# Rotary attention: scores computed a second time with keys on partitions, and four heads summed in one bank

## The chip, the cores and the metric

The kernel runs on one core of a Trainium2 chip. The metric is the device time of one execution in microseconds (us). The core has TensorE (PE; its weight loads are listed as PEld), VectorE (DVE), ScalarE (ACT), GpSimd (POOL) and SyncE (SP), which run side by side and wait for each other through semaphores. TensorE writes only to PSUM, eight banks of 512 f32 columns on 128 partitions.

## The reference

Four token sequences of 576 tokens (64 image patches and 512 text tokens) with 64 features go through four layers, each of an attention and a feed-forward part. The change lies in the attention of the second layer's feed-forward block, a causal softmax attention with rotary positions, 4 heads of 16 features (k and v are shared by two heads each):

```python
q = q * cos + _rotate_half(q) * sin
k = k * cos + _rotate_half(k) * sin
scores = jnp.einsum('bhtd,bhsd->bhts', q, k) / jnp.sqrt(jnp.float32(HD))
scores = jnp.where(causal[None, None], scores, jnp.float32(-1e+30))
att = jax.nn.softmax(scores, axis=-1)
y = jnp.einsum('bhts,bhsd->bhtd', att, v).transpose(0, 2, 1, 3).reshape(Bx, Tx, Cx)
x = x + y @ wo.T
```

The other parts (a linear attention, a retrieval attention over a table of keys, a Toeplitz layer by transforms, the experts after this attention, a sparse attention, a tree of small layers, a sigmoid attention, experts) are not touched.

## The kernel before

The kernel is a row of stages. A stage opens one or more blocks; in a block every engine runs its own list of instructions in the order in which it is written, and a barrier of all engines ends the block. There is no planner: the order within each list and the semaphores between lists are written out by hand. Tokens lie on partitions: a sequence is 5 tiles (CH) of 128 tokens, the last of 64 (TAIL), and there are 20 tiles (T) in all. SEQ is 576, P 128, D 64, BANK 512, HD 16.

`rotary_experts_stage` (line 2058) norms the input, makes qkv by one product, turns q and k by the rotary tables on DVE, and then runs these stages in turn:

- `stack_parts_stage` (line 2010): every q and k value is cut into bf16 parts, and six of them are laid side by side, so that a bf16 product over 6 x 16 = 96 (PARTS) features gives nearly f32 scores. ACT, POOL and DVE share the copies; POOL waits for the first cast before its own four.
- `causal_attention_stage` (line 926), called "rot_soft", with `CausalAttention` (from line 691). For each of 16 heads (4 sequences of 4) POOL copies q, k and v of the head into small tiles. TensorE turns q and k (line 785) so that features lie on partitions, and DVE copies them out of PSUM (line 801). For each tile c of 128 queries TensorE makes the scores against the (c+1) x 128 keys up to them (lines 811 and 813), DVE adds the mask and takes the row's maximum in one instruction (line 913) and scales it (line 916), ACT takes the exponential with the row's sum (line 881), TensorE turns the exponentials block by block (line 823, f32), ACT copies them to SBUF (line 871), and TensorE weighs v: the turned exponentials are the stationary operand and 16 columns of v the moving one (line 836). DVE divides by the sum (lines 893, 896). TensorE's list interleaves the next head's turn and first scores with this head's. DVE, ACT and TensorE run these lists as hardware loops over pairs of heads.
- a fill of the lower half of yT (line 688), and `turn_stage` (line 301), which turns the attention's result, so that features lie on partitions (lines 315, 324, 332).
- `product_stage` (line 336) for the output projection, which adds to core.xn (lines 354, 2099).

Another attention, `RetrievedAttention` (line 1005), is a subclass of `CausalAttention` with f32 scores and 64 features; it stays as it is.

Of the kernel before, what the change touches and what calls it, by code (L numbers as in the profile page):

```python
# [21 lines left out]
BF16 = mybir.dt.bfloat16  # L22
ACT = mybir.ActivationFunctionType
AX = mybir.AxisListType

P = 128
B = 4
PATCHES = 64
TEXT = 512
SEQ = PATCHES + TEXT  # L30
D = 64
CH = 5
PAD = CH * P
TAIL = SEQ - 4 * P
T = B * CH
COLS = T * P
BANK = 512
GROUPS = COLS // BANK
LN_EPS = 1e-5
NEG = -1e30  # L40
# [641 lines left out]
def set_stage(nc, name, fills):  # L682

    with nc.Block() as block:
        @block.gpsimd
        def _(pool):
            for ap, value in fills:
                nc.gpsimd.memset(ap, value)


class CausalAttention:
# [213 lines left out]
    def dve_head(self, dve, steps, n, u, more, carry, out_of, out_before=None):  # L905
# [15 lines left out]
                self.dve_turn(dve, n + 1, 1 - u, c == 2)  # L921
        if not more:
            self.dve_norm(dve, steps, n, u, out_of)


def causal_attention_stage(nc, core, name, sources, out, heads, d, scale, parts=None):

    with Stage(nc, name) as st:  # L930
        A = CausalAttention(nc, core, st, d, scale, parts=parts)
        widths = (A.dq, A.dq, d)
        vec = st.sem("vector_steps")
        A.begin()
        pairs = heads // 2
        views = lambda b, h: [of[:, bass.ds(b * CH, CH), bass.ds(h * stride + start, w)]
                              for (of, stride, start), w in zip(sources, widths)]
        out_of = lambda b, h: (lambda lo, hi, r: out[0:r, bass.ds(b * CH + lo, hi - lo), bass.ds(h * d, d)])

        def walk(engine, pair):  # L940

            def sequence(b, first=False, last=False):
                for j in range(pairs):
                    pair(b, j, first and j == 0, last and j == pairs - 1)

            sequence(0, first=True)
            with engine.Fori(1, B - 1) as b:
                sequence(b)
            sequence(B - 1, last=True)

        with nc.Block() as block:
            @block.gpsimd
            def _(pool):
                with pool.Fori(0, B) as b:
                    with pool.Fori(0, pairs) as j:
                        for u in range(2):
                            A.pool_fetch(pool, b * heads + j * 2 + u, u, *views(b, j * 2 + u))

            @block.tensor
            def _(pe):  # L960
                A.pe_start(pe, 0, 0)
                with pe.Fori(0, B * pairs - 1) as m:
                    for u in range(2):
                        A.pe_head(pe, m, u, True)
                for u in range(2):
                    A.pe_head(pe, B * pairs - 1, u, u == 0)

            @block.scalar
            def _(act):
                with act.Fori(0, B * pairs) as m:  # L970
                    for u in range(2):
                        A.act_head(act, 2 * m + u, u)

            @block.vector
            def _(dve):
                steps = Steps(dve, vec)

                def pair(b, j, first, last):
                    n, h = b * heads + j * 2, j * 2

                    steps.before, steps.count = A.STEPS * n - (0 if first else 2), 0
                    if first:
                        A.dve_start(dve, n, 0)
                    before = None if first else out_of(b, h - 1) if h else out_of(b - 1, heads - 1)
                    A.dve_head(dve, steps, n, 0, True, not first, out_of(b, h), before)
                    A.dve_head(dve, steps, n + 1, 1, not last, True, out_of(b, h + 1), out_of(b, h))

                walk(dve, pair)


KEYS = 64
# [924 lines left out]
Q_HEADS = 4  # L1916
HD = D // Q_HEADS
# [87 lines left out]


PARTS = 6 * HD


def stack_parts_stage(nc, qkv, q_parts, k_parts):  # L2010


    with Stage(nc, "parts") as st:
# [9 lines left out]
        with nc.Block() as block:  # L2023
# [13 lines left out]

            @block.gpsimd
            def _(pool):
                pool.wait_ge(cast, 1)  # L2040
                place(nc.gpsimd.tensor_copy, q_parts, 4, 0, 0)
                for column in (0, 2, 5):
                    place(nc.gpsimd.tensor_copy, k_parts, column, 0, 1)
# [14 lines left out]
def rotary_experts_stage(nc, core, I, norm):  # L2058


    with Stage(nc, "rot") as st:
        spare = st.sb("spare", [P, T, D])
        with Stage(nc, "rot_attn") as at:
# [13 lines left out]
            with Stage(nc, "rope") as rt:  # L2077
                vec = rt.sem("vector_steps")
                with nc.Block() as block:
                    @block.vector  # L2080
                    def _(dve):
# [3 lines left out]
                        for b in range(B):  # L2085
                            for lo, table in parts:
# [2 lines left out]
                                    table[:, :, :].unsqueeze(2).to_broadcast([P, CH, 2 * Q_HEADS, HD]), ALU.mult))  # L2089
                        steps.settle()  # L2090
                        steps.do(nc.vector.tensor_tensor(qkv[:, :, 0:2 * D], qkv[:, :, 0:2 * D], qkv[:, :, 2 * D:4 * D], ALU.add))
            q_parts, k_parts = (at.sb(n, [P, T, Q_HEADS * PARTS], BF16) for n in ("q_parts", "k_parts"))
            stack_parts_stage(nc, qkv, q_parts, k_parts)
            causal_attention_stage(nc, core, "rot_soft", [(q_parts, PARTS, 0), (k_parts, PARTS, 0), (qkv, HD, 4 * D)], qkv,
                                   Q_HEADS, HD, HD ** -0.5, parts=PARTS)
            set_stage(nc, "rot_padding", [(yT[D:P, :], 1.0)])
            turn_stage(nc, core, "rot_turn", [(yT, D, lambda t: qkv[:, t, 0:D])])
            product_stage(nc, core, "rot_proj", [(lambda t: yT[:, t * P:(t + 1) * P], w_out[:, :])], D,
                          lambda t0, t1, made: nc.vector.tensor_tensor(core.xn[:, t0:t1, :], core.xn[:, t0:t1, :], made, ALU.add))
        router, weight = st.sb("router", [P, T, EXPERTS]), st.sb("weight", [P, T, EXPERTS])  # L2100
# [849 lines left out]
```

## Time and profile before

| | us |
|---|---|
| median of three runs | 4470.99 (4460.36 to 4479.04) |
| the profiled execution | 4491.15 |
| its span | 4489.0 |
| TensorE busy | 3640.8 (81%) |
| DVE busy | 2651.9 (59%) |
| ACT busy | 1496.4 (33%) |
| POOL busy | 359.1 (8%) |

Shares of busy time are means over a row of very different stages. The rotary attention is about a twentieth of the span, so it is read from the stretch in which it runs. Busy time of TensorE counts products in flight, and products overlap: where the time that a product occupies TensorE matters, it is the distance from its start to the next one's. "PEclk" and the granted clock of a stretch are TensorE's clock as a share of full speed: 1.00 is 2.4 GHz, 0.50 is 1.2 GHz.

### The profile page before, as it was taken

The page shows a single profiled execution, that of the slowest core. Times are in us where ns is not written, and L with a number is a line of the kernel's source. Part 1 is how long each engine was busy: PE and PEld are TensorE (multiplying, and loading weights), DVE is VectorE, ACT ScalarE, POOL GpSimd, SP SyncE. Part 2 cuts the span into 40 slices and gives each one's busy share as a digit, 9 for nine tenths or more (in the row PEclk, how much of TensorE's full clock was granted, in tenths as well). Part 3 has the DMA queues.
Part 4 walks back from the last instruction along what each step waited for, and adds up shares of the span by engine and source line. Part 5 has one row for each costly group of instructions (what it writes and reads, how often), then busy time and mean ns, then how long its engine had stood idle before and what let it go on. Part 6 is the DMA issues. An engine that isn't in the chain of part 4 may idle for free. (4 is left out here: it accounts for less than half of the span.)

```text
span 4489.0 us, 57158 instructions
## 1 busy us (share of the span) xinstructions
PE 3640.8 (81%) x16965; PEld 2172.9 (48%) x17110; DVE 2651.9 (59%) x7758; ACT 1496.4 (33%) x2931; POOL 359.1 (8%) x351
## 2 busy tenths in 40 slices
PE   5528889999999999999799868848869372799867
PEld 4325545544454554444466645437747252344354
DVE  3369878777887877555333322144344555899812
ACT  2203444444444444444333330034432133100023
POOL 1000000000000000000000001111000000355500
PEclk8569999999999999999878877975579665899968
DMA  0102334443443444443000020000010002100000
GB/s 7 52 10 76 102 87 102 87 91 86 101 92 83 101 88 91 107 104 71 24 19 20 21 79 0 0 4 1 1 31 0 1 0 54 43 0 0 0 7 5
DMA packets 140950, 207.83 MB, mean 46 GB/s; under 512 B 35104, under 2 KB 119657, under 8 KB 135469
## 3 DMA queue, kind: packets, MB, share of 16 engines
q1 hardware_dynamic: 140717, 205.03, 19.1%
q8 instruction: 108, 1.77, 0.2%
q14 instruction: 125, 1.02, 0.1%
HBM read 115.66 MB, written 10.03 MB: 28 GB/s over the span
## 5 line engine op out<-in xcount | busy, mean ns | idle before, releaser
L1256 PE MATMUL psum<-pk_W,pk_kv 128*128 128x512 f32 (+1 forms) x2560 | 1203.8, 552 | 10.0 <-issue 9.8
L1487 DVE SCALAR_TENSOR_TENSOR pk_W<-psum,pk_E 128x512 f32<-128x512 f32 (+1 forms) x1280 | 810.5, 633 | 440.3 <-ACT pk_E L1354 407.2
L1354 ACT ACTIVATE pk_E<-psum 128x512 f32<-128x512 f32 (+1 forms) x1280 | 708.8, 554 | 1005.0 <-PE psum L1246 1003.1
L1256 PEld LDWEIGHTS psum<-pk_W,pk_kv 128*128 128x128 f32 x2560 | 465.4, 191 | 173.7 <-issue 27.0
L1245 PE MATMUL psum<-pk_stack,pk_spread 128*128 128x512 bf16 (+1 forms) x1171 | 420.4, 359 | 80.0 <-DVE pk_W L1487 53.6
L1246 PE MATMUL psum<-pk_stack,pk_spread 128*128 128x512 bf16 (+1 forms) x1280 | 459.4, 359 | 17.7 <-DMA pk_stack<-pk_marks 9.5
L2480 PE MATMUL psum<-tree_w,tree_x 128*128 128x512 bf16 x1692 | 381.0, 380 | 112.9 <-PEq L120 90.7
L1245 PEld LDWEIGHTS psum<-pk_stack,pk_spread 128*128 128x128 bf16 x1280 | 125.1, 98 | 444.8 <-DVE pk_W L1487 349.4
L2480 PEld LDWEIGHTS psum<-tree_w,tree_x 128*128 (+1 forms) x1728 | 168.2, 99 | 312.0 <-issue 121.3
L2551 DVE COPY_PREDICATED leaf_acc<-leaf_path,psum 128x512 f32<-128x512 uint32 x468 | 310.4, 729 | 5.1 <-PE psum L2480 2.8
L1246 PEld LDWEIGHTS psum<-pk_stack,pk_spread 128*128 128x128 bf16 x1280 | 125.7, 98 | 241.8 <-issue 232.0
L1220 PEld LDWEIGHTS psum<-pk_ranked,pk_onehot 128*128 128x128 bf16 x2304 | 168.3, 149 | 115.4 <-issue 102.8
L1220 PE MATMUL psum<-pk_ranked,pk_onehot 128*128 128x128 bf16 x2304 | 172.1, 230 | 56.9 <-DVE pk_onehot L1445 56.9
L1190 POOL TENSOR_TENSOR pk_parts<-pk_left,pk_parts 128x512 bf16<-128x512 f32 (+1 forms) x40 | 44.0, 1100 | 1814.9 <-ACT pk_parts L1325 1814.9
L1441 DVE TENSOR_TENSOR pk_onehot<-pk_idf,pk_count 128x2048 bf16<-128x2048 bf16 x144 | 175.4, 1218 | 1.2 <-PE psum L1220 0.6
L295 PE MATMUL psum<-ident,xn 128*64 128x128 f32 x160 | 34.2, 407 | 171.7 <-DVEq L269 157.6
L881 ACT ACTIVATE peer_probs<-peer_probs,peer_stat 128x128 f32<-128x128 f32 (+4 forms) x160 | 96.3, 602 | 222.9 <-DVE peer_stat L916 222.7
L811 PE MATMUL psum<-peer_kv,peer_qT_padded 128*128 128x128 f32 (+4 forms) x320 | 163.3, 603 | 5.9 <-DVE peer_v L1051 3.5
L913 DVE CUSTOM_DVE_ANT_0 peer_probs<-psum,peer_mask 128x128 f32<-128x128 f32 (+4 forms) x160 | 85.9, 537 | 116.2 <-PE psum L811 106.2
L1957 PE MATMUL psum<-moe_x,moe_w 128*85 x480 | 113.8, 388 | 43.6 <-PEq L120 42.3
L1061 PE MATMUL psum<-peer_v,peer_pT 128*128 128x64 f32 (+2 forms) x960 | 139.4, 289 | 0.0
L1061 PEld LDWEIGHTS psum<-peer_v,peer_pT 128*128 128x128 f32 (+2 forms) x960 | 123.7, 202 | 20.7 <-issue 15.3
(513 smaller groups left out, 4970.1 us busy)
## 6 DMA issues: line engine op xcount, KB each, us to landing
pk_kv<-in_kv SPq DMA_DIRECT2D x40, 2048.0 KB, 7.8
pk_stack<-pk_parts SPq DMA_DIRECT2D x768, 64.0 KB, 2.5
pk_stack<-pk_marks SPq DMA_DIRECT2D x256, 64.0 KB, 2.6
peer_kv<-peer_kept SPq DMA_DIRECT2D x32, 288.0 KB, 2.8
peer_kept<-pk_made SPq DMA_DIRECT2D x32, 256.0 KB, 2.1
tree_weights_x<-in_tree_w SPq DMA_DIRECT2D x32, 256.0 KB, 4.6
pk_stack<-pk_parts SPq DMA_DIRECT2D x192, 32.0 KB, 2.0
dft_cos<-in_cos SPq DMA_DIRECT2D x1, 2596.5 KB
```

The costliest lines, as they stand in the source:

```text
L811: last = nc.tensor.matmul(ps[0:r, bank, 0:min(w, BANK)], q, self.kT[:, u, 0:min(w, BANK)], start=True, stop=True)
L1061: last = nc.tensor.matmul(ps[0:r, 1, c * d:(c + 1) * d], self.pT[0:k, self.pT_at[c] + m * r:self.pT_at[c] + (m + 1) * r], self.v1[0:k, u, ...
L1220: last = nc.tensor.matmul(ps[:, 6 + h // 4, h % 4 * P:(h % 4 + 1) * P], onehot[:, h % 2, :, :, r], ranked[:, r, :], start=(r == 0), stop=( ...
L1245: nc.tensor.matmul(ps[:, n % 2, 0:N], spread[:, 1, c % 2, :], of, start=True, stop=True)
L1246: nc.tensor.matmul(ps[:, 2 + n % 2, 0:N], spread[:, 0, c % 2, :], of, start=True, stop=True).then_inc(x_made, 1)
L1256: nc.tensor.matmul(ps[:, 4, 0:N], kv[:, k % 2, c, :], W[:, n % 3, 0:N], start=(c == 0), stop=(c == CHUNKS - 1)).then_inc(acc_done, 1)
L1354: nc.scalar.activation(E[:, n % 2, 0:width(k)], ps[:, 2 + n % 2, 0:width(k)], ACT.Exp).then_inc(e_made, 1)
L1441: steps.do(nc.vector.tensor_tensor(onehot[:, h % 2, :, :, :], idf[:, :, h, :].unsqueeze(2).to_broadcast([P, 2, KEYS, TOP]), count64[:, :, ...
L1487: nc.vector.scalar_tensor_tensor(W[:, n % 3, 0:width(k)], ps[:, n % 2, 0:width(k)], TOP + 0.5, E[:, n % 2, 0:width(k)], ALU.is_gt, ALU.mul ...
L1957: last = nc.tensor.matmul(ps[0:HALF, 3 * which + u % 3, :], w[:, lo:lo + HALF], x[:, bass.ds(g * BANK, BANK)], start=(k == 0), stop=(k == 2))
L2480: last = nc.tensor.matmul(ps[:, n % BANKS, :], x[:, bass.ds(t * P, P)], w[:, c * BANK:(c + 1) * BANK], start=(k == 0), stop=(k == len(prod ...
L2551: ins = nc.vector.copy_predicated(acc[:, u, level + 1, :, :], over(mask.bitcast(U32), D), bank)
```

## The change

`causal_attention_stage` goes, and with it the fill and the turn stage behind it. `rotary_attention_stage` takes its place. For each head n:

- TensorE turns q and k as before, straight from the stacked parts, which now have a stride of 128 (Q_STRIDE) instead of 96; ACT copies them out of PSUM (two copies) instead of DVE.
- First scores, queries on partitions, and DVE's masked maximum as before, but with nothing after it: DVE's instruction writes its sums to a scratch tile and keeps the maximum.
- DVE writes the negative maximum as two bf16 pieces into two of the 32 spare columns of the stacked q parts (`piece`); the spare columns of k hold 1. TensorE turns these q tiles again (`turn_peaks`), and DVE copies the rows 96 to 127 into the turned q (`copy_peaks`). A contraction over all 128 rows then gives score minus maximum.
- Second scores with keys on partitions (`score_turned`): three banks per head hold all key blocks against the queries from them on; the causal mask is added by TensorE as a product of an identity with a bf16 mask. ACT takes three exponentials of 512 columns, PSUM to SBUF.
- Weighing (`weigh`): v is the stationary operand, 128 columns wide (its head's 16 columns at the head's place among 64, zeros beside them, and ones at 64 columns further), and the exponentials are the moving operand in f32. All four heads of a sequence accumulate in bank 1, with values in rows 0 to 63 and sums in rows 64 to 127, already turned. The first 64 queries go to a piece of bank 2.
- After each fourth head DVE takes the reciprocal of the sums and multiplies into yT (`norm`); the first weighing of the next sequence waits for it.

The lists are written out over all 16 heads in place of the hardware loops. POOL fills v for two sequences at a time and sets the spare columns and yT in `stack_parts_stage`, ahead of its wait for the cast.

```diff
-def causal_attention_stage(nc, core, name, sources, out, heads, d, scale, parts=None):
...
+Q_STRIDE = P
+LEAD = SEQ - BANK
...
+    return (
+        [*scores(a[:, :], slice(0, P), slice(LEAD, SEQ)), *masked(a[:, 0:P - LEAD], LEAD + LEAD, P - LEAD)],
+        [*scores(b[0:LEAD, 0:LEAD], slice(0, LEAD), slice(0, LEAD)), *scores(b[LEAD:P, 0:LEAD], slice(BANK, SEQ), slice(BANK, SEQ)),
+         *masked(b[:, 0:LEAD], 0, LEAD), *scores(b[:, LEAD:BANK], slice(P, 2 * P), slice(P, SEQ)), *tri(b, LEAD)],
+        [*scores(c[:, 0:SEQ - 2 * P], slice(2 * P, 3 * P), slice(2 * P, SEQ)), *tri(c, 0),
+         *scores(c[:, SEQ - 2 * P:BANK], slice(3 * P, 4 * P), slice(3 * P, SEQ)), *tri(c, SEQ - 2 * P)])
...
+SCORE_ORDER = (4, 3, 2, 1, 0)
+SCORE_BANKS = (6, 6, 7, 6, 7)
+SCORE_FREE = (0, 1, 1, 2, 3)
...
+                def score(n, j):
...
+                    if n >= 1 or j >= 1:
+                        pe.wait_ge(peaked, CH * n + SCORE_FREE[j])
...
+                def turn_peaks(n):
+                    b, h = divmod(n, Q_HEADS)
+                    pe.wait_ge(pieced, n + 1)
...
+                def score_turned(n):
+                    pe.wait_ge(peaks_copied, n + 1)
...
+                        if n >= 1:
+                            pe.wait_ge(exped, 3 * n - 2 + i)
+                        for to, k, q, start, stop in group:
+                            last = nc.tensor.matmul(to, k, q, start=start, stop=stop)
+                        last.then_inc(st_made, 1)
...
+                def weigh(n, some):
...
+                    for i in some:
+                        pe.wait_ge(exped, 3 * n + (1, 2, 3, 3, 2)[i])
+                        if i == 0:
+                            pe.wait_ge(v_copied, V_COPIES * (b + 1))
+                            if h == 0 and b:
+                                pe.wait_ge(normed, 2 * b)
+                        cols, lhsT, rhs = parts[i]
+                        last = nc.tensor.matmul(ps[:, 1, cols], lhsT, rhs, start=(h == 0 and i == 0), stop=(h == Q_HEADS - 1 and i == 4))
+                        if i == 0:
+                            pe.wait_ge(exped, 3 * n + 2)
+                            pe.wait_ge(qk_copied, 2 * min(n + 3, heads))
+                            nc.tensor.matmul(ps[:, 2, LEADS + h * LEAD:LEADS + (h + 1) * LEAD], v[0:LEAD, b % 2, h, 0, :],
+                                             pT[0:LEAD, n % 2, 1, 0:LEAD], start=True, stop=True)
...
+                turn(0)
+                turn(1)
+                for j in range(CH):
+                    score(0, j)
+                for n in range(heads):
+                    more = n + 1 < heads
+                    if n:
+                        weigh(n - 1, (0,))
+                    if more:
+                        score(n + 1, 0)
+                    turn_peaks(n)
+                    if n:
+                        weigh(n - 1, (1,))
+                    if more:
+                        score(n + 1, 1)
+                        score(n + 1, 2)
+                    score_turned(n)
+                    if n + 2 < heads:
+                        turn(n + 2)
+                    if more:
+                        score(n + 1, 3)
+                    if n:
+                        weigh(n - 1, (2, 3, 4))
+                    if more:
+                        score(n + 1, 4)
+                weigh(heads - 1, (0, 1, 2, 3, 4))
...
+                for n in range(heads):
+                    for i in range(3):
+                        act.wait_ge(st_made, 3 * n + i + 1)
+                        if n >= 2:
+                            act.wait_ge(weighed, n - 1)
+                        nc.scalar.activation(pT[:, n % 2, i, :], ps[:, 3 + i, :], ACT.Exp, scale=scale).then_inc(exped, 1)
+                    if n + 2 < heads:
+                        copy(n + 2)
...
+                def norm(b):
+                    dve.wait_ge(weighed, Q_HEADS * (b + 1))
...
+                    nc.vector.reciprocal(inverse[:, LEAD:SEQ], ps[D:P, 1, :]).then_inc(inverted, 1)
...
+                    nc.vector.tensor_tensor(yT[0:D, b * PAD + LEAD:b * PAD + SEQ], ps[0:D, 1, :], inverse[:, LEAD:SEQ], ALU.mult
...
+                for n in range(heads):
+                    more = n + 1 < heads
+                    if more:
+                        peak(n + 1, 0)
+                    copy_peaks(n)
+                    if more:
+                        for j in range(1, CH):
+                            peak(n + 1, j)
+                        piece(n + 1)
+                    if n and n % Q_HEADS == 0:
+                        norm(n // Q_HEADS - 1)
+                norm(B - 1)
...
+                nc.gpsimd.memset(head(q_parts[:, :, :])[:, :, :, PARTS:Q_STRIDE], 0.0)
+                nc.gpsimd.memset(head(k_parts[:, :, :])[:, :, :, PARTS:Q_STRIDE], 1.0)
+                nc.gpsimd.memset(yT[:, :], 0.0)
                 pool.wait_ge(cast, 1)
...
-            q_parts, k_parts = (at.sb(n, [P, T, Q_HEADS * PARTS], BF16) for n in ("q_parts", "k_parts"))
-            stack_parts_stage(nc, qkv, q_parts, k_parts)
-            causal_attention_stage(nc, core, "rot_soft", [(q_parts, PARTS, 0), (k_parts, PARTS, 0), (qkv, HD, 4 * D)], qkv,
-                                   Q_HEADS, HD, HD ** -0.5, parts=PARTS)
-            set_stage(nc, "rot_padding", [(yT[D:P, :], 1.0)])
-            turn_stage(nc, core, "rot_turn", [(yT, D, lambda t: qkv[:, t, 0:D])])
+            q_parts, k_parts = (at.sb(n, [P, T, Q_HEADS * Q_STRIDE], BF16) for n in ("q_parts", "k_parts"))
+            stack_parts_stage(nc, qkv, q_parts, k_parts, yT)
+            rotary_attention_stage(nc, core, q_parts, k_parts, qkv, yT)
```

## Rows read from the trace of the kernel before

**Rows 1.** The page, part 2: TensorE's granted clock in 40 slices.
```profile
PEclk8569999999999999999878877975579665899968
```
**Rows 2.** Stretches: rotary attention, retrieved attention, retrieval; span, busy time (instructions), clock, DMA.
```profile
3036.00:3228.00 192.00, 178.63 (x966) 154.65 (x966) 78.35 (x366) 95.45 (x263) 19.28 (x43) 0.50 0.00 0
2160.00:2620.00 460.00, 416.95 (x2237) 282.08 (x2236) 174.90 (x738) 173.07 (x518) 0.00 (x0) 0.83 0.07 20
1780.00:2100.00 320.00, 316.68 (x980) 142.12 (x997) 172.24 (x250) 155.66 (x266) 8.10 (x7) 1.00 0.47 103
```
**Rows 3.** Timeline: start, duration, instruction; one copy in two neighbouring heads.
```profile
3099.79 0.41 DVE L801 COPY rot_soft_kT<-psum 96x512 bf16<-96x512 bf16 x1
3111.79 0.41 DVE L801 COPY rot_soft_kT<-psum 96x512 bf16<-96x512 bf16 x1
```
**Rows 4.** Waits in 3036 to 3228: total, times, longest.
```profile
DVE rot_soft_probs L913 <- PE psum L811: 70.2, 31, 4.3
```
**Rows 5.** Groups in 3028 to 3228: count, busy us, mean ns, idle before.
```profile
L836 PEld LDWEIGHTS psum<-rot_soft_v,rot_soft_pT 128*128 128x128 f32 x320 | 75.3, 331 | 2.9 <-issue 2.9
L785 PE MATMUL psum<-rot_soft_ident,rot_soft_qk 128*96 128x128 bf16 x128 | 17.0, 314 | 29.7 <-POOL rot_soft_qk L767 29.7
L913 DVE CUSTOM_DVE_ANT_0 rot_soft_probs<-psum,rot_soft_mask 128x128 f32<-128x128 f32 (+4 forms) x80 | 43.2, 540 | 73.3 <-PE psum L811 70.2 <-issue 1.9 <-PE psum L813 0.4
```
**Rows 6.** Timeline of TensorE in the retrieval's dense stretch.
```profile
1799.75 0.38 PE L1246 MATMUL psum<-pk_stack,pk_spread 128*128 128x512 bf16 x1
1799.97 1.02 PE L1256 MATMUL psum<-pk_W,pk_kv 128*128 128x512 f32 x2
1800.82 0.38 PE L1245 MATMUL psum<-pk_stack,pk_spread 128*128 128x512 bf16 x1
```
**Rows 7.** Groups in the whole span, shapes apart.
```profile
L1061 PE MATMUL psum<-peer_v,peer_pT 128*128 128x64 f32 x640 | 101.0, 295 | 0.0
L1220 PE MATMUL psum<-pk_ranked,pk_onehot 128*128 128x128 bf16 x2304 | 172.1, 230 | 56.9 <-DVE pk_onehot L1445 56.9
L354 PE MATMUL psum<-sparse_w_o,xnT 128*128 128x64 f32 x40 | 8.8, 422 | 0.9 <-PEq L308 0.9
L1354 ACT ACTIVATE pk_E<-psum 128x512 f32<-128x512 f32 x1024 | 611.0, 597 | 820.5 <-PE psum L1246 820.4
L2346 DVE RECIPROCAL sparse_soft_stat<-sparse_soft_stat 128x8 f32<-128x8 f32 x20 | 4.1, 203 | 0.7
L232 DVE RECIPROCAL norm_stat<-norm_stat 128x20 f32<-128x20 f32 x8 | 2.2, 278 | 2.3 <-ACT norm_stat L282 2.3
```
**Rows 8.** Timeline around the stage, from the stacked parts to the projection.
```profile
3014.00 2.34 ACT L2026 ACTIVATE parts_part<-rot_attn_qkv 128x2560 bf16<-128x2560 f32 x1 [9.63 <-PEq L2079]
...
3016.39 3.90 POOL L2021 COPY rot_attn_q_parts<-parts_part 128x1280 bf16<-128x1280 bf16 x1 [92.19 <-ACT parts_part L2026]
...
3020.24 6.23 POOL L2021 COPY rot_attn_k_parts<-parts_part 128x1280 bf16<-128x1280 bf16 x3
...
3027.14 0.48 DVE L2021 COPY rot_attn_k_parts<-parts_part 128x1280 bf16<-128x1280 bf16 x1
3029.07 1.06 POOL L755 MEMSET rot_soft_mask<- 128x1152 f32 x1 [2.59 <-POOLq L100]
...
3030.29 1.15 POOL L759 TENSOR_SCALAR_AFFINE_SELECT rot_soft_mask<-rot_soft_mask 128x1152 f32<-128x1152 f32 x1 [0.16 <-POOL rot_soft_mask L755]
...
3227.31 0.30 DVE L896 TENSOR_TENSOR rot_attn_qkv<-psum,rot_soft_stat 128x64 f32<-128x64 f32 x2
3227.89 2.23 POOL L688 MEMSET rot_attn_yT<- 64x2560 f32 x1 [22.16 <-ACTq L684]
...
3235.16 4.65 PE L354 MATMUL psum<-rot_attn_w_out,rot_attn_yT 128*128 128x64 f32 x40 [0.93 <-PEq L308]
```
**Rows 9.** Timeline and stretch (columns of Rows 2) of a TensorE gap in the transforms.
```profile
2751.07 4.87 PE L1748 MATMUL psum<-dft_a,dft_cos 128*128 128x192 f32 x18 [1.92 <-ACT dft_vf L1769]
...
2752.00:2755.50 3.50, 3.50 (x13) 3.50 (x13) 3.46 (x3) 0.00 (x0) 3.50 (x2) 0.52 0.02 5
```

More of the change, by code:

```diff
@@ L923, in dve_head @@
             self.dve_norm(dve, steps, n, u, out_of)
-def causal_attention_stage(nc, core, name, sources, out, heads, d, scale, parts=None):
[L930 to L988, printed above, removed]
@@ L2007, with causal_masks @@
 PARTS = 6 * HD
-def stack_parts_stage(nc, qkv, q_parts, k_parts):
+Q_STRIDE = P
+LEAD = SEQ - BANK
+def causal_masks(nc, pool, steps, mask, turned_mask):
+    steps.do(nc.gpsimd.memset(mask[:, :], 0.0))
+    steps.do(nc.gpsimd.affine_select(out=mask[:, :], in_=mask[:, :], compare_op=ALU.is_ge, fill=NEG,
+                                     base=PAD - P, pattern=[[-1, 2 * PAD - P]], channel_multiplier=1))
+    twin, corner = turned_mask[:, 0:LEAD], turned_mask[:, LEAD:LEAD + P]
+    steps.do(nc.gpsimd.memset(turned_mask[:, :], 0.0))
+    steps.do(nc.gpsimd.affine_select(out=corner, in_=corner, compare_op=ALU.is_ge, fill=NEG,
+                                     base=0, pattern=[[1, P]], channel_multiplier=-1))
+    steps.do(nc.gpsimd.affine_select(out=twin, in_=twin, compare_op=ALU.is_ge, fill=NEG,
+                                     base=0, pattern=[[1, LEAD]], channel_multiplier=-1))
+    steps.do(nc.gpsimd.affine_select(out=twin, in_=twin, compare_op=ALU.is_ge, fill=0.0,
+                                     base=LEAD - 1, pattern=[[0, LEAD]], channel_multiplier=-1))
+    steps.do(nc.gpsimd.affine_select(out=twin, in_=twin, compare_op=ALU.is_ge, fill=NEG,
+                                     base=LEAD, pattern=[[1, LEAD]], channel_multiplier=-1))
@@ new lines, in turned_scores, with scores, masked @@
+def turned_scores(bank_of, k, q, mask16, ident16, ones16=None, shift=None):
+    a, b, c = bank_of
+    def scores(to, keys, queries):
+        yield to, k[:, keys], q[:, queries], True, False
+        if shift is not None:
+            yield to, ones16[:, 0:to.shape[0]], shift[:, queries], False, False
+    def masked(to, at, n):
+        yield to, ident16[:, :], mask16[:, at:at + n], False, True
+    tri = lambda bank, at: masked(bank[:, at:at + P], LEAD, P)
+    return (
[4 more added lines that the diff above has]
+         *scores(c[:, SEQ - 2 * P:BANK], slice(3 * P, 4 * P), slice(3 * P, SEQ)), *tri(c, SEQ - 2 * P)])
@@ L2013, in stack_parts_stage @@
+def stack_parts_stage(nc, qkv, q_parts, k_parts, yT):
     with Stage(nc, "parts") as st:
```

147 lines of the change are left out of this document (added).

## The prediction

> **What bounds the kernel now.** I looked first for the stage of the change: the rotary attention lies at 3029 to 3235 us of the span, where the clock line of the page shows two slices at half [rows 1]. The table of stretches then gives the attention proper: 192 us in which TensorE has work in flight for 178.6 us, at a granted clock of 0.50 throughout, that is 1.2 GHz, while DVE is busy for 78 us and ACT for 95 [rows 2]. The timeline shows what a head costs: one recurring copy starts 12.0 us apart in neighbouring heads, so 16 heads are 192 us [rows 3]. The waits say the same from the other side: DVE waits 70.2 us in total for score products [rows 4]. TensorE bounds the stage, and not with arithmetic: its largest group are weight loads of 128x128 f32 at 331 ns, each for 16 columns [rows 5]. So the change is judged by TensorE time per head, by the clock that the new mix is granted, and by what it puts into TensorE's way.
>
> **What a head costs TensorE after it.** Per head there are 15 transposes (eight full ones of q and k, two short, five of the peaks), first scores of 128+256+384+512+576 = 1856 bf16 columns, turned scores with their masks of 2112 bf16 columns in 11 products, and six weighings with f32 operands: 512+448+320+192 columns, and two of 64.
> At the full clock, f32 first. In the dense stretch of the retrieval a 512-column f32 product (two records) starts at 1799.97 and the next product at 1800.82, 0.85 us; a bf16 one of 512 columns takes 0.22 [rows 6]. The four wide weighings are 1472 columns: 2.44 us. The two narrow ones are four records; the 64-column records of the retrieved attention take 101.0/640 = 0.158 us: 0.63. Turned scores: 2112 columns at 0.22 per 512, 0.91, and 0.25 more (estimate) because seven of the eleven are too short to cover their weight load. First scores: 0.80. Transposes: 172.1/2304 = 0.075 each [rows 7], 1.12. Sum 6.15 us; I add 0.35 for waits that don't close up: **6.5 us a head**. Bounds: 5.3, if narrow products cost their columns alone, and 7.5, if each of some ten waits costs 0.1 to 0.15.
> At the half clock the columns double, a short f32 record costs 75.3/320 = 0.235 and a transpose 17.0/128 = 0.133 [rows 5]: weighing 5.8, turned scores 2.1, scores 1.6, transposes 2.0, waits 0.4, together 11.9, as much as now. The clock decides whether the change is worth anything.
> I take the full clock. The retrieval, f32 products of 512 columns with bf16 ones of 512 between them, ran at 1.00 through 320 us; the retrieved attention, scores of 128 to 512 columns and weighings of 64, at 0.83; the present stage at 0.50 [rows 2]. In its forms the new head is nearest to the first.
>
> **The other engines beside it.** DVE keeps its five peaks, 43.2/80 = 0.54 us each [rows 5], with their read-outs and waits 3.6 us a head; the peak copy is 0.46 (the 512-column bf16 copy takes 0.41 [rows 3]), the two pieces 0.5: 4.6. ACT has three exponentials of 0.60 [rows 7], a copy of 1024 columns (1.0, estimate at 0.8 ns for each column beyond those 512) and its tail of 0.3: 3.1. Both fit under 6.5. Walking one turn of the loop from the last first-score of head n: TensorE weighs the first part (1.1 with its lead), in which DVE finishes the last peak and the pieces; the scores of head n+1 and the turned peaks go out; the 0.74 us weighing of 448 columns and DVE's first peak and peak copy run beside each other to about 3.1; turned scores, turn, and the rest of the weighing fill TensorE to 6.4. Nothing on TensorE waits for long.
>
> **What surrounds the heads.** *Start.* The masks are 1.06 + 1.15 [rows 8] and five small steps up to 0.3 each, 3.7; their cast 0.4; two turns 2.8 with a copy 1.3 between; scores and peaks of head 0 alternating on two banks, 3.6 plus four scores at half clock of 0.6, 6.0; pieces 0.5: 14.7 us. Head 0's turn of the loop, at half clock without weighing, 11.9 - 5.8 = 6.1.
> *Norm.* New and unseen is a reciprocal of 512 columns. The 8-column one takes 203 ns and the 20-column one 278 [rows 7], 6.25 ns a column: 3.35 us (estimate; 0.7 if it ran at the rate of the peaks, 0.54 us for 371 columns, and that is the other bound). I take 3.35, since it is the same operation. With the 64-column one (0.55), a reduction and two products (1.2) it is 5.3 with its waits. For three of four sequences it sits on the path: the first weighing of the next sequence waits for it at the head of TensorE's queue, with all scores behind it, and DVE has the next peak copy behind it. TensorE is then out of work for 5.3 + 1.0 (last peak, pieces). After a gap of 1.92 us in the transform stage (next product at 2751.07) the clock stood at 0.52 for the stretch to 2755.5 [rows 9]; 3.5 us at half cost 1.75, and I take 2.5 because this gap is longer. Each norm: 8.8, three: 26.4 (bounds 9 and 30).
> *Sum of the stage.* 14.7 + 6.1 + 14 x 6.5 = 91.0 + 2.7 (half clock as weighing begins, estimate by the same row) + 4.6 (last turn of the loop: weighing, peaks, turned scores) + 1.2 (last exponentials) + 3.1 (last weighing) + 5.3 (last norm) + 26.4 = 155.1 us, against 3029.07 to 3227.61 = 198.5 now [rows 8]: 43.4 less.
> *Behind it.* The padding, the turn stage and their two barriers are 3227.61 to 3235.16, 7.55 us [rows 8]; a barrier of about 0.7 is left: 6.8 less. But the output projection now starts after 5.3 us without TensorE work instead of after transposes: at half it costs what its twin in the sparse stage costs, 8.8 against 4.6 [rows 7]: 4.2 more.
> *Ahead of it.* POOL gets three fills before it waits for the cast: one of 2560 f32 columns takes 2.23 [rows 8], two of 2560 bf16 columns 1.1 to 2.2 each; from about 3014.0, where the stage's first copy starts, they last to some 3019.4, 3.0 past the 3016.39 at which POOL's first copy starts now [rows 8]. POOL ended at 3026.5 and DVE at 3027.6, so about 2.2 more (0 to 5).
> **Sum:** 43.4 + 6.8 - 4.2 - 2.2 = 43.8 us. The profiled execution took 4491.15 (span 4489.0 and 2 around it), so 4447 for it; it lies 20 above the median of the runs, 4470.99, and against that the same gain gives **4427 us**.
>
> **Rivals.** (1) *The clock stays at half.* Then 14.7 + 6.1 + 14 x 11.9 = 166.6, last turn 8.7, 1.2, 5.8, 5.3, and three norm waits of 6.3: 227.3 us, 28.8 more than now; with the rest (-6.8 + 4.2 + 2.2) 28.4 slower, 4499 us. For it: the half clock through all of the stage today, with TensorE busy as now. Against it: neither of the two stretches with wide f32 products stayed there [rows 2]. It decides from about 9.6 us a head, where the gain is gone. Chance 0.06.
> (2) *The clock swings.* The head hands over between engines at some ten places, two banks for five scores. The retrieved attention swings under such hand-overs, 0.83 in the mean [rows 2]. A head is then 6.5/0.83 = 7.8 us, 14 heads 18 us more: 4445. Chance 0.14. The Trainium skill ("TensorE: Matmul & The Clock Gate", "A second HAM failure mode: psum-queue depth-cycling") speaks for this one: a kernel that cycles through PSUM banks idles the engine in small bits, and its clock goes back and forth. By that rule 4445 would be the forecast; the retrieved attention's row agrees with it, the retrieval's row (eight banks in turn, 1.00) does not.
> (3) *The chain of hand-overs is longer than TensorE's work.* Peaks 3.6, four score latencies of 0.4, pieces 0.5, turned peaks 0.6 and their copy 0.5 are 6.8 end to end, just above 6.5; were the wide f32 weighings to stand between a peak and its next score in the queue (0.74 and 0.85 each, three such waits), a head is about 9: 35 more, 4462, no change. Against it: the walk above, in which each weighing lies beside a peak. Chance 0.12.
> (4) *The norm is short* (reciprocal 0.7) and the clock survives it: three times 5.5, the last one's 2.7 and the projection's 4.2 less, 4403. Chance 0.08.
> The forecast keeps 0.60, its own range 4408 to 4448 (5.7 to 7.2 us a head with the bounds of the norm).
>
> **How the numbers follow.** Three runs of the kernel before lie 19 us apart, so 0.5% (22 us, below 4448.6) is about what can be told from no change. Faster: nearly all of the forecast (0.58), half of (2), and (4): 0.73. Same: (3), the rest of (2) and a little of the forecast: 0.20. Slower: (1) and a worse (3): 0.07. The range cuts a tenth on either side: 4400 to 4468.
>
> **What would show it.** In the profile after: a granted clock near 1.0 in the stretches between norms, with dips after each fourth head; recurring instructions 6.5 us apart; TensorE's largest wait the one for the norm, some 6 us, three times; reciprocals of about 3.4 us; POOL's first copy of the parts near 3019 instead of 3016.4. It is wrong if heads are over 8 us apart at the full clock (3), if the stretch shows 0.5 (1), or if the reciprocal is under 1 us (4).

## The result and the profile after

The changed kernel took **4430.5 us** (median of 5 runs, 4422.5 to 4438.2) beside 4470.99 for the kernel before (median of 5, 4460.4 to 4490.7): ratio 0.9898, 95% interval 0.9874 to 0.9922. 4427 was forecast. The profiled execution has a span of 4428.8 us.

The two profiled spans differ by 60.2 us, but not all of that is the change. The stage's first copy starts at 3014.00 before [rows 8] and at 3001.59 after, so 12.4 us of it lie in stages that the diff leaves alone, and 4.5 more behind it. From that copy to the end of the output projection it is 3239.81 - 3014.00 = 225.81 us before and 3184.08 - 3001.59 = 182.49 after: **43.3 us less**, where 43.8 was forecast. I use such stretches below; they vary far less than whole runs (the first of them, from that copy to the mask's fill, takes 15.07 us in the kernel before and 15.07 or 15.08 in each run below that builds on it).

TensorE's clock in 40 slices, as in [rows 1]; two executions differ by a tenth or two in slices that the change doesn't touch, so finer views are needed:
```profile
PEclk8569999999999999999879887977779675999968
```
The table of stretches (columns of [rows 2]): heads, the wait for a norm, the time behind it, and the stage as a whole.
```profile
3046.00:3064.00 18.00, 18.00 (x121) 10.58 (x121) 9.60 (x35) 8.11 (x15) 0.00 (x0) 1.00 0.00 1
3064.00:3070.30 6.30, 0.08 (x1) 0.02 (x1) 5.84 (x9) 0.00 (x0) 1.36 (x8) 0.78 0.00 0
3070.30:3077.30 7.00, 6.99 (x19) 2.77 (x19) 1.92 (x5) 0.00 (x0) 0.00 (x0) 0.50 0.01 2
3036.00:3168.00 132.00, 113.28 (x648) 62.41 (x647) 67.19 (x204) 40.35 (x74) 2.72 (x16) 0.88 0.00 1
```
Read it against the 0.50 throughout of [rows 2]: the heads run at 1.00 with TensorE never idle; in the norm's wait it does nothing for 6.2 us, and the next 7 us of its work go at half the clock.

The timeline: the peak copy of two neighbouring heads, 6.75 us apart (12.0 in [rows 3]); then the first norm and the weighing that waits for it:
```profile
3046.30 0.46 DVE L2200 COPY rot_soft_qk<-psum 32x576 bf16<-32x576 bf16 x1
3053.05 0.47 DVE L2200 COPY rot_soft_qk<-psum 32x576 bf16<-32x576 bf16 x1
...
3064.92 3.36 DVE L2207 RECIPROCAL rot_soft_inverse<-psum 64x512 f32<-64x512 f32 x1
...
3069.96 0.21 DVE L2213 TENSOR_TENSOR rot_attn_yT<-rot_soft_lead,rot_soft_inverse 64x64 f32<-64x64 f32 x1
...
3070.31 2.05 PE L2115 MATMUL psum<-rot_soft_pT,rot_soft_v 128*128 128x512 f32 x2 [6.23 <-DVE rot_attn_yT L2213]
```
The waits from 3016 to 3176. DVE waits for scores nearly as long as before (70.2 us [rows 4], now 37.1 and 29.5 on two lines), but between norms behind a TensorE at the full clock; and TensorE has a wait of its own, three times:
```profile
DVE rot_soft_masked L2187 <- PE psum L2080: 37.1, 44, 2.3
...
DVE rot_soft_masked L2187 <- PE psum L2082: 29.5, 16, 9.1
...
PE psum L2115 <- DVE rot_attn_yT L2213: 18.6, 3, 6.2
```
The timeline around the stage, which answers to [rows 8]: POOL's three fills, its first copy, DVE's last one, the mask, the last norm's end and the projection.
```profile
3001.57 2.24 POOL L2266 MEMSET rot_attn_q_parts<- 128x2560 bf16 x1 [90.94 <-POOLq L2308]
3001.59 2.34 ACT L2252 ACTIVATE parts_part<-rot_attn_qkv 128x2560 bf16<-128x2560 f32 x1 [9.63 <-PEq L2308]
...
3008.09 1.24 POOL L2247 COPY rot_attn_q_parts<-parts_part 128x1280 bf16<-128x1280 bf16 x1
...
3014.85 1.53 DVE L2247 COPY rot_attn_k_parts<-parts_part 128x1280 bf16<-128x1280 bf16 x1
...
3017.83 1.06 POOL L1949 MEMSET rot_soft_mask<- 128x1152 f32 x1 [1.79 <-SPq L2040]
...
3174.78 0.20 DVE L2213 TENSOR_TENSOR rot_attn_yT<-rot_soft_lead,rot_soft_inverse 64x64 f32<-64x64 f32 x1
3175.31 8.77 PE L354 MATMUL psum<-rot_attn_w_out,rot_attn_yT 128*128 128x64 f32 x40 [5.61 <-PEq L2040]
```

### The profile page after: what moved, and what is told of

Same layout as the page of the kernel before. It is cut to its first block and busy times, and to the rows that moved or that the text cites. A ratio compares the mean times of both kernels' runs of the same rounds, so it can differ in the third digit from the quotient of the medians.

```text
span 4428.8 us, 55552 instructions
## 1 busy us (share of the span) xinstructions
PE 3578.2 (81%) x16818; PEld 2073.3 (47%) x16818; DVE 2649.8 (60%) x7617; ACT 1444.5 (33%) x2746; POOL 351.8 (8%) x354
## 5 line engine op out<-in xcount | busy, mean ns | idle before, releaser
L1180 PE MATMUL psum<-pk_stack,pk_spread 128*128 128x512 bf16 (+1 forms) x1280 | 462.0, 361 | 90.3 <-DVE pk_W L1422 54.2
L1181 PE MATMUL psum<-pk_stack,pk_spread 128*128 128x512 bf16 (+1 forms) x1280 | 459.3, 359 | 0.0
L2749 POOL TENSOR_TENSOR leaf_acc<-leaf_acc,leaf_of_level 128x512 f32<-128x512 f32 x90 | 90.5, 1039 | 536.6 <-DVE leaf_acc L2777 536.6
```

What stands on the lines that cost most here:

```text
L1180: nc.tensor.matmul(ps[:, n % 2, 0:N], spread[:, 1, c % 2, :], of, start=True, stop=True)
L1181: nc.tensor.matmul(ps[:, 2 + n % 2, 0:N], spread[:, 0, c % 2, :], of, start=True, stop=True).then_inc(x_made, 1)
```

## The experiments

The yardstick is "the stage": from the mask's fill to the projection's end, 210.74 us before [rows 8], 166.25 after. The peak copies of the changed kernel lie 6.75 us apart in ordinary heads, but 14.6 across each norm and 8.6 to 9.2 in the head after it, though TensorE waits for nothing there. Around the first norm:
```profile
3059.80 0.46 DVE L2200 COPY rot_soft_qk<-psum 32x576 bf16<-32x576 bf16 x1
...
3074.42 0.46 DVE L2200 COPY rot_soft_qk<-psum 32x576 bf16<-32x576 bf16 x1
...
3083.04 0.47 DVE L2200 COPY rot_soft_qk<-psum 32x576 bf16<-32x576 bf16 x1
```
A ratio below is the run's time to that of the kernel before; a time without a range is of a single run. Theory: TensorE's products set the head; a norm costs its wait and, behind it, the half clock. Rivals: hand-overs set the head; the time behind a norm is work that DVE has to catch up on.

**Weighing in bf16** (exponentials and values carry fewer bits).
```diff
-        v = st.sb("v", [P, 2, Q_HEADS, CH, P])
+        v = st.sb("v", [P, 2, Q_HEADS, CH, P], BF16)
...
-        pT = st.sb("pT", [P, 2, 3, BANK])
+        pT = st.sb("pT", [P, 2, 3, BANK], BF16)
```


> The changed kernel with the weighing in bf16: v and the exponentials are kept in bf16 instead of f32, all else as it is, so the exponentials lose precision. Theory (TensorE's work sets the time of a head, 6.75 us in the changed kernel): the wide weighings fall from 0.85 us per 512 columns to 0.22 and the two narrow ones from four records to two, 2.2 us less TensorE per head, so heads come 4.6 to 5.2 us apart, where DVE's 4.6 us begins to bind, and the attention stage falls from 157 to some 128 to 134 us. Rival (the chain of hand-overs from score to peak, pieces, turned peaks and their copy is what sets the time): heads stay 6.3 us or more apart and the stage loses under 8 us.


Measured: 4379.6 us (median of seven runs of the kernel before on the same chip: 4477.7), heads 5.2 us apart, the stage 133.5.
```profile
3019.66 0.46 DVE L2200 COPY rot_soft_qk<-psum 32x576 bf16<-32x576 bf16 x1
3024.85 0.46 DVE L2200 COPY rot_soft_qk<-psum 32x576 bf16<-32x576 bf16 x1
```
```profile
3018.00:3033.00 15.00, 13.49 (x113) 7.23 (x114) 10.44 (x38) 7.51 (x15) 0.00 (x0) 1.00 0.00 1
```
With fewer records in the weighing and all hand-overs left in place, the head falls by 1.55 us: in the changed kernel TensorE sets it, not the hand-overs. The 2.2 us that were to go did not all go: at 5.2 TensorE is no longer full (13.49 of 15.00 us at the full clock), so there the hand-overs take part.

**Fillers in the norm's wait.** Fillers are products into a bank that nobody reads.
```diff
                             if h == 0 and b:
+                                pe.wait_ge(peaked, CH * (n + 2))
+                                for _ in range(24):
+                                    nc.tensor.matmul(ps[:, 6, :], ident16[:, :], qk[:, n % 4, 1, 0:BANK], start=True, stop=True)
                                 pe.wait_ge(normed, 2 * b)
...
                 weigh(heads - 1, (0, 1, 2, 3, 4))
+                for _ in range(26):
+                    nc.tensor.matmul(ps[:, 6, :], ident16[:, :], qk[:, (heads - 1) % 4, 1, 0:BANK], start=True, stop=True)
```


> The changed kernel with 24 products of 128x512 bf16 into a free bank ahead of each wait for the norm, and 26 after the last weighing; nothing reads them. Theory (each norm costs 9.9 us: a wait of 6.2 and 3.6 for the half clock that follows, and the projection runs at half for the same reason): the wait stays 6.2, the clock stays at 1.00, the heads after it come 6.75 apart instead of 8.6 to 9.0, the turn with the norm takes 13 instead of 14.6, the projection 4.7 instead of 8.8; 15 us less in all. Rival (the time after the norm is the filling of an emptied chain, whatever the clock): nothing gained behind the norm, at most the 4.1 of the projection.


Measured: ratio 0.9884 (0.9855 to 0.9914), which whole runs can't tell from the change's 0.9898; but the stage takes 151.34 us, 14.9 less than the changed kernel. The stretch of all norms, and the projection:
```profile
3021.00:3154.00 133.00, 130.05 (x788) 73.09 (x788) 73.87 (x212) 39.55 (x73) 2.72 (x16) 1.00 0.00 1
```
```profile
3149.12 4.65 PE L354 MATMUL psum<-rot_attn_w_out,rot_attn_yT 128*128 128x64 f32 x40 [0.30 <-PEq L2040]
```
The wait is as long as before (13.1 us across a norm, 6.35 above a head), but every other head takes 6.75 and the projection 4.65: what lay behind a norm was the clock, 3.4 to 4.0 us each, and 4.1 in the projection.

**Early release.** The sums are copied out of PSUM, and the reciprocal follows in six pieces between the peaks of later heads.
```diff
-                                pe.wait_ge(normed, 2 * b)
+                                pe.wait_ge(freed, 2 * b)
...
+                    nc.vector.tensor_copy(held[:, :], ps[:, 1, :]).then_inc(freed, 1)
...
+                            if j in (2, 3):
+                                slot()
```


> The changed kernel with a norm that first copies the four heads' sums out of PSUM (512 columns, 0.7 us, and the 0.4 us reduction) and then lets TensorE go on; the reciprocals follow in six pieces, two per head, between DVE's peaks, from SBUF. The last norm is as it was. Theory: TensorE waits 2.4 us per norm instead of 6.2, 11 us less in all; the clock still falls behind it, as it did after a gap of 1.9 us in the transforms. If it does not, 22 us less. Rival (DVE has no room between its peaks): heads with pieces of the reciprocal in them are 0.6 to 1.2 us longer, which gives back 5 to 10 us.


Measured: ratio 0.9882 (0.9849 to 0.9914), the stage 147.71 us, 18.5 less than the changed kernel: between the two numbers expected. TensorE's gap shrank to 1.9 us, and heads with pieces still take 6.75.
```profile
3074.43 1.84 PE L2117 MATMUL psum<-rot_soft_pT,rot_soft_v 128*128 128x512 f32 x2 [1.88 <-DVE rot_soft_lead L2215]
...
3106.52 1.10 PE L2117 MATMUL psum<-rot_soft_pT,rot_soft_v 128*128 128x512 f32 x2 [1.90 <-DVE rot_soft_lead L2215]
```
The same two records took 1.84 us behind the first norm and 1.10 behind the second (1.52 behind the third, after 1.86 us): the clock fell after one gap and not after another of the same length.

**Both together**, with 8 fillers instead of 24 in each norm's wait, and the 26 ahead of the projection.


> The changed kernel with the early release (the sums copied out of PSUM, reciprocals in six pieces between the peaks of later heads), 8 filler products ahead of each wait of the weighing and 26 ahead of the projection. Theory (a norm costs its wait, and then the half clock that the wait leaves behind; both can be taken away and the pieces fit beside TensorE): clock 1.00 through the whole stage, heads 6.75 us with and without pieces, the turns with a norm 8.5 to 9 us, the projection 4.65 us; mask fill to projection's end 137 to 140 us instead of 166.25 (147.7 with the early release alone, less 1.8 + 2.1 in the heads behind norms 1 and 3, 1.2 + 0.9 in their turns and 4.1 in the projection). Time 4400 to 4406 us. Rival (the clock falls for some other reason than TensorE's idle time, so that it falls now and then with the fillers too): dips stay behind at least one norm, 143 to 150 us, about 4410.


Measured: 4403.6 us (4398.8 to 4409.3), ratio 0.9849 (0.9826 to 0.9872), the stage 139.47: 26.8 less than the changed kernel, 26.9 between the two medians, though taken on two chips. Heads across a norm take 9.06, the heads between and behind them 6.75.
```profile
3036.00:3150.00 114.00, 111.24 (x682) 63.12 (x690) 74.59 (x221) 38.36 (x71) 2.72 (x16) 1.00 0.00 1
```
The rival, a clock that falls for other reasons than an idle TensorE, is not borne out: with the gaps filled it stayed at 1.00 behind all three norms.

**All of it**: that kernel, bf16 weighing, and POOL's three fills issued in the stage before.
```diff
-                nc.gpsimd.memset(head(q_parts[:, :, :])[:, :, :, PARTS:Q_STRIDE], 0.0)
...
+                        nc.gpsimd.memset(spare(q_parts[:, :, :]), 0.0)
```


> As the one with early release and fillers, and besides the weighing takes exponentials and values in bf16 (one record of a product instead of two; they carry fewer bits), and GpSimd's three fills of the parts stage are issued in the stage before. Theory: fills out of the way bring the start of the parts to the mask's fill back from 16.24 to about 15.1 us. Heads without pieces 5.2 us; in heads with two pieces of 0.69 us VectorE (4.6 us of work per head, 1.4 of pieces) becomes the bound, 5.9 to 6.2 us; mask fill to projection's end 112 to 121 us (138 less 15 heads x 1.55, plus up to 3 x 3 x 0.8). Rival 1 (TensorE still sets the heads with pieces): all heads 5.2, 112 us or less. Rival 2 (the fills cost nothing, the 1.2 us come from the longer copies of VectorE): 16.2 us stays.


Measured: 4385.9 us (4369.7 to 4400.3), ratio 0.9813 (0.9787 to 0.9840), the stage 119.55, within the 112 to 121 of the theory. The first part to the mask's fill is 3000.30 - 2985.23 = 15.07 us, as before, instead of 16.24: the fills cost 1.2.
```profile
2985.23 2.34 ACT L2300 ACTIVATE parts_part<-rot_attn_qkv 128x2560 bf16<-128x2560 f32 x1 [9.63 <-PEq L2354]
...
2987.60 2.83 DVE L2322 TENSOR_TENSOR parts_rest<-rot_attn_qkv,parts_part 128x2560 f32<-128x2560 f32 x1 [2.86 <-ACT parts_part L2300]
2987.63 3.90 POOL L2295 COPY rot_attn_q_parts<-parts_part 128x1280 bf16<-128x1280 bf16 x1 [5.20 <-ACT parts_part L2300]
...
3000.30 1.06 POOL L1949 MEMSET rot_soft_mask<- 128x1152 f32 x1 [2.59 <-SPq L2042]
```
Heads between norms take 5.2 to 5.9 us (5.5 in most): under the 5.9 to 6.2 of the theory with DVE as the bound, over the 5.2 of its rival. Neither engine is full there (TensorE first, DVE third):
```profile
3050.00:3100.00 50.00, 41.28 (x325) 21.69 (x330) 42.67 (x131) 21.62 (x40) 1.86 (x8) 1.00 0.00 1
```

**The kernel before, at the full clock.** How much of the old head's 12.0 us was the clock? First, fillers ahead of the turns of keys.
```diff
         if self.parts:
+            for _ in range(4):
+                nc.tensor.matmul(ps[:, 0, :], self.ident16[:, :], wide, start=True, stop=True)
             bank = ps[:, 0, :].bitcast(BF16)
```


> The kernel before with work added: four products of 128x512 bf16, which nothing reads, ahead of each of the two turns of a head, eight per head. Theory (the old stage stands at 12.0 us a head because it runs at the half clock): if the added products bring the clock up, heads fall to 8 to 9 us although TensorE has 1.7 us more to do, and the stage to 130 to 145 us. Rival (the gain comes from fewer and wider instructions, the clock counts for little): heads rise by 1.7 to 3.4 us, the stage to 220 to 250 us. If the clock stays at half, both say 15.4 us a head, 247 us.


Measured: 4505.6 us, heads of 12.2 to 14.7 at a mean clock of 0.68. The forecast missed; the stage, 232.6, lies in the 220 to 250 of its rival, by which the clock counts for little. But with a clock that swings the run says nothing of a steady full clock, on which the two differ.
```profile
3098.00:3200.00 102.00, 90.93 (x521) 64.56 (x520) 37.17 (x171) 43.12 (x121) 10.96 (x24) 0.68 0.00 0
```
With ten in each turn instead of four:


> The kernel before with 10 filler products of 512 columns in each turn of keys, 20 in a head (4.3 us at the full clock, 8.5 at half), so that TensorE is busy enough for its clock to hold; one look at how much of the old head's 12.0 us was the clock and how much the hand-overs. Theory (most of the gain is structure, the clock gives a small part): at a clock of 1.00 a head takes 15 to 15.5 us, that is about 11 without the fillers, against 6.75 in the changed kernel. Rival (the old head was long because of the half clock): 11 us or less with the fillers, about 6.5 to 7 without them. If the clock stays below 0.9 in the stage the run doesn't decide.


Measured: 4553.5 us, heads of 17.0 to 17.2 at 0.70; undecided by its own condition (a clock under 0.9). But its stretches show where the clock goes: after two microseconds in which TensorE had 0.64 us of work in flight it is at half, through fillers and all.
```profile
3103.00:3105.00 2.00, 0.64 (x7) 0.52 (x7) 1.54 (x7) 1.30 (x4) 0.00 (x0) 1.00 0.01 4
3106.00:3115.00 9.00, 8.78 (x37) 5.60 (x39) 1.12 (x7) 2.02 (x8) 1.37 (x3) 0.50 0.00 0
```
So the same twenty were put where TensorE waits, ahead of each turn of exponentials:
```diff
...
+            for _ in range(4):
+                nc.tensor.matmul(ps[:, self.TURN_BANK[c], :], self.ident16[:, :], self.wide, start=True, stop=True)
         pe.wait_ge(self.exped, self.BEGIN + CH * n + c + 1)
```


> The kernel before with 4 filler products of 512 columns ahead of each of the five turns of exponentials of a head (20 a head, 4.3 us of TensorE at the full clock), where TensorE waits for ACT; earlier fillers in the turns of keys left the clock swinging between 0.67 and 0.74. Theory (the old head's 12.0 us are in good part its half clock, but its hand-overs keep it longer than the new one even at 1.00): clock near 1.00, a head of 11 to 13 us with fillers, its own products 5.5 to 7 us of TensorE. Rival 1 (the products themselves, weight loads for 16 columns, are the length at either clock): own products 9 us or more at 1.00. Rival 2: the clock swings as before, 14 to 17 us a head, undecided.

> The same with 8 fillers ahead of each turn, 40 a head, 8.6 us at the full clock: slower by itself, only to hold the clock so that the old products can be timed at 1.00. Theory: clock 1.00 from the second head on, a head of 15 to 17 us, its own products 5.5 to 7 us of TensorE (the rest fillers and waits). Rival (products set by weight loads that the clock doesn't shorten): own products 9 us or more.


Measured: with 20 a head 4438.6 us (before beside it 4482.4), heads of 10.6 us, the stage 192.5; with 40 a head 4516.6 and 14.8. Both heads are shorter than forecast (11 to 13, 15 to 17). In both the clock is 1.00 and TensorE full; the first fences are of 20 (two heads lie between the copies), the others of 40 (one head).
```profile
3024.75 0.41 DVE L801 COPY rot_soft_kT<-psum 96x512 bf16<-96x512 bf16 x1
...
3045.93 0.41 DVE L801 COPY rot_soft_kT<-psum 96x512 bf16<-96x512 bf16 x1
```
```profile
3040.00:3180.00 140.00, 139.93 (x1072) 97.08 (x1071) 62.36 (x292) 77.14 (x217) 15.32 (x34) 1.00 0.00 0
```
```profile
3072.64 0.41 DVE L801 COPY rot_soft_kT<-psum 96x512 bf16<-96x512 bf16 x1
...
3087.46 0.41 DVE L801 COPY rot_soft_kT<-psum 96x512 bf16<-96x512 bf16 x1
```
```profile
3060.00:3240.00 180.00, 180.00 (x1228) 113.22 (x1226) 60.83 (x284) 73.70 (x200) 15.32 (x34) 1.00 0.00 0
```
Twenty fillers more cost 14.81 - 10.59 = 4.22 us, 0.211 each, so without any the products of an **old head are 10.59 - 4.22 = 6.37 us of TensorE at the full clock**, no more than the new head's 6.75. Twice 6.37 is 12.7, over the 12.0 us of the old head: not all of it can double at half the clock, but its products alone are enough to fill the old head there. Then fewer of them:


> The kernel before with 2 fillers ahead of each of the five turns of exponentials, 10 a head (2.1 us at the full clock). With 20 and 40 a head the clock stood at 1.00, the head took 10.6 and 14.8 us and TensorE had no idle time: own products 6.3 to 6.4 us. Theory (at the full clock the old head needs no more TensorE than the new one, and the change's gain in the heads is the clock): if the clock holds, heads of 8.4 to 9 us and the stage from the mask's fill to the projection's end 156 to 165 us, as long as the changed kernel's 166; the time then 4415 to 4435 us. Rival 1 (the hand-overs of the old head are a chain of 10 us or more that the fillers only filled): heads stay at 10 or more at a clock of 1.00, 185 us or more. Rival 2: with so few the clock swings and a head takes 9.5 to 12.

> The same with 1 filler ahead of each turn, 5 a head (1.1 us): where the clock is lost again. If it holds, heads of 7.4 to 8.5 us, and a chain of hand-overs longer than TensorE's 6.3 + 1.1 would be seen as idle time of TensorE; if it swings, 9 to 12 us at a clock between 0.55 and 0.9.


Measured with 10 a head: 4430.1 us (4425.6 to 4436.2), ratio 0.9896 (0.9855 to 0.9938), which can't be told from the change's 0.9898. The stage can: it takes 181.2 us, where 156 to 165 was expected and the changed kernel takes 166.25. From the first copy to the projection's end ten fillers win 225.81 - 196.22 = 29.6 us, the change 43.3. At the full clock a head takes 9.1 to 10.0, where 8.4 to 9 was expected: TensorE has 0.6 us a head without work, so the hand-overs begin to show. In 3120 to 3140 the clock fell, though TensorE had work in flight for 19.69 of 20.00 us; why there is not shown.
```profile
3040.00:3100.00 60.00, 56.53 (x454) 39.64 (x452) 30.93 (x147) 37.73 (x105) 8.22 (x18) 1.00 0.00 0
3120.00:3140.00 20.00, 19.69 (x125) 13.59 (x125) 9.26 (x42) 10.06 (x30) 2.74 (x6) 0.74 0.00 0
```
With 5 a head: 4463.2 us, clock 0.76, heads of 9.2 to 13.3, the stage 195.8.
```profile
3040.00:3180.00 140.00, 130.91 (x878) 99.25 (x877) 64.94 (x306) 78.35 (x218) 18.06 (x40) 0.76 0.00 0
```

## Why the prediction was right

The mechanism held: TensorE's work sets the new head, its clock is full between norms, and it dips behind each norm. That the sum fits to 0.5 us is partly luck: heads and norms cost 7.3 us more than forecast, the start, the end and what lies around the stage 6.8 less.

**The bound and the clock: right, and now measured.** The prediction said that at half clock the new head would cost 11.9, "as much as now", and that the clock decides. No run held the new head at half clock, so the 11.9 is not measured (the 0.235 in it for a short f32 record is the time of a weight load [rows 5], not of a product). The fillers in the old kernel show the other half of it: at the full clock the old products need 6.37 us, the new ones 6.75. At the full clock the change spares TensorE nothing; its 5.25 us a head come from a form of the work in which the clock holds and no hand-over holds TensorE up. How the 5.25 split between the two is open: the old head would not stay at 1.00 without fillers, and with ten it takes 9.1 to 10.0 there, more than the 6.37 + 2.11 = 8.48 of its work. With five fillers the old head's clock was 0.76, with none 0.50, and with ten it did not hold throughout; the new head, between norms, leaves TensorE no wait.

**The head: 6.75 against 6.5.** Fourteen times 0.25 is 3.5 us more. In 3046 to 3064 TensorE is busy for 18.00 of 18.00, so the 0.35 set for waits doesn't show as idle time. Counted from start to start in the head from 3045.87, the six weighings take 3.55 us, where 2.44 + 0.63 = 3.07 was set, and all the rest 3.20, where 3.08 was set. So the term that was too small is the weighing. An example is the weighing of 512 columns, with 1.01 us to the next product instead of 0.85, and the narrow pair behind it, with 0.36 instead of 0.32:
```profile
3050.42 1.08 PE L2115 MATMUL psum<-rot_soft_pT,rot_soft_v 128*128 128x512 f32 x2
3051.43 0.43 PE L2119 MATMUL psum<-rot_soft_pT,rot_soft_v 64*128 64x64 f32 x2
3051.79 0.40 PE L2080 MATMUL psum<-rot_soft_qk 128*64 128x512 bf16 x1
```
Whether these are longer products or short waits behind a product still in flight is not shown.

**The norm: right in its parts, short in its wake.** The reciprocal took 3.36 us (3.35 forecast from the small ones [rows 7]), the wait 6.2 (6.3). The half clock behind it was put at 2.5 and measures 3.4 to 4.0: three norms cost 30.2 instead of 26.4, just past the upper bound of 30. Of that, 19.1 is the wait and 11.1 the clock.

**Start and end: 5.2 us too dear.** The stage to the last norm's end measures 157.15 (3017.83 to 3174.98) against 155.1. Take off the 3.5 of the heads and the 3.8 of the norms, and all the rest is 5.2 under its forecast: the first peak copy comes 14.8 us after the mask's fill, the first turn of the loop takes 6.95, where 6.1 and a further 2.7 for the clock had been set, and the last two copies lie 5.35 apart, where a full head was counted.

**Behind it: right.** The projection takes 8.77 us (8.8 forecast, its twin's time [rows 7]), after 0.33 for the barrier instead of 0.7.

**Ahead of it: 1.2 instead of 2.2.** POOL's fills took 2.2 us each and its first copy came 6.5 us after the start instead of 2.4. The copy made up for it: 1.24 us where [rows 8] has 3.90, because the latter began beside a subtraction of DVE and this one found DVE idle. The Trainium skill ("SBUF — State Buffer", "SBUF: two separate sides") says that a GpSimd operation that reads SBUF and a VectorE operation with two SBUF inputs lock each other out of a shared pair of ports; the 2.66 us of difference agree with that: the run with the fills moved shows the 3.90 again, beside a subtraction of 2.83.

**The rivals.** The clock did not stay at half (1). It does average 0.88 over the stage, but by dips behind norms, not by the swing of (2): between norms it is 1.00. The rule of the Trainium skill that was weighed there ("TensorE: Matmul & The Clock Gate", "A second HAM failure mode: psum-queue depth-cycling") therefore does not describe this stage, though the new head's first scores alternate between two banks. (The retrieval's dense stretch, called "eight banks in turn" there, goes through five in its loop: lines 1245, 1246 and 1256 write banks 0 and 1, 2 and 3 by turns, and 4.) The chain of (3) is out by the bf16 run: with every hand-over left, its head takes 5.2. The norm of (4) is not short; with early release and fillers it costs 2.3 us, and the 4403.6 us of that kernel lie close to the 4403 that (4) gave for a short one.

## What to carry to other kernels

Where TensorE is nearly always busy at a clock of 0.50, time a version with filler products in its waits before a rewrite: ten a head here won 29.6 us where the new layout wins 43.3, though their places matter (twenty in two lumps made the kernel slower). Price a wait of TensorE with the half clock behind it: 6.2 us of waiting cost 3.7 more, and eight fillers and an early release of PSUM took both away but for 2.3. A reciprocal over 512 columns belongs off the path, in pieces.

## What the hardware showed that I had not expected

Twenty fillers a head gave heads of 17.1 us in two lumps and of 10.6 spread over the five waits: where the work stands counts more than how much there is. A gap of 1.88 us brought the clock down and one of 1.90 did not, in the same kernel. From 64 columns (0.55 us) to 512 (3.36) the f32 reciprocal costs 6.3 ns for each further column, as between the two small ones of the forecast (6.25).
